# A chain of convolutions on one core: the first image's tables moved into its second convolution, the last image's mix and stores reordered

## The reference, cut to what matters

```python
# L0: attention over the 4096 pixels of an image, then three convolutions
qkv = batchnorm(x) @ w_qkv + b_qkv            # q, k centred, squared, normalised
attn = (v + q2 @ (k2.T @ v) / 64) @ w_ln + b_ln
y = leaky_relu(conv1x1(concat(attn, x), w1))  # conv1, 96 -> 96
y = leaky_relu(conv3x3(y, w2))                # conv2, 96 -> 96
x = conv1x1(y, w3) + x                        # 96 -> 48
# L1: separable convolution
x = batchnorm(pointwise(depthwise3x3(relu(x))))
# L2: weights mixed per image from 4 experts
rw = sigmoid(mean(x, (1, 2)) @ Wr + br)       # routing, 4 numbers
h = relu(bn1(x @ mix(rw, Wpw)))               # expansion, 48 -> 192
h = relu(bn2(depthwise3x3(h, mix(rw, Wdw))))  # 192 channels
x = bn3(h @ mix(rw, Wpwl)) + x                # projection, 192 -> 48
# L3: like L1, with its own weights
```

## Time and profile before

| | us |
|---|---|
| median of 3 runs (1068.31 to 1069.65) | 1069.26 |
| the profiled execution | 1068.75 |
| its span, first to last instruction | 1066.9 |
| TensorE busy in the span | 983.1 (92%) |
| VectorE busy | 877.0 (82%) |
| ScalarE busy | 473.4 (44%) |
| GpSimd busy | 94.7 (9%) |

### The profile page before, as it was taken

One profiled execution on the slowest core, in us unless ns is written; L12 is line 12 of the kernel. 1 busy time (PEld: TensorE's weight loads), 2 busy tenths in 40 slices (PEclk: granted clock), 3 DMA queues, 4 the chain that ended last, 5 costly groups with the idle time before them and its releaser, 6 DMA issues.

```text
span 1066.9 us, 14764 instructions
## 1 busy us (share of the span) xinstructions
PE 983.1 (92%) x4598; PEld 625.9 (59%) x4598; DVE 877.0 (82%) x1231; ACT 473.4 (44%) x813; POOL 94.7 (9%) x120
## 2 busy tenths in 40 slices
PE   5689879998999999998999999998999999998986
PEld 3456655665665666665665566665665676654624
DVE  6762579998699968999699978999599978997980
ACT  3311445255624635345533636355632646333522
POOL 0210002001300103001300003001200013000000
PEclk9799989999999999999999999999999999998998
DMA  5242815185526565175534656175533756145215
GB/s 73 50 122 50 142 31 143 30 134 127 115 76 96 106 130 139 35 120 126 126 81 82 119 116 151 35 120 112 123 98 71 131 118 150 36 91 118 60 30 102
DMA packets 129520, 104.48 MB, mean 98 GB/s; under 512 B 97903, under 2 KB 98772, under 8 KB 129492
## 3 DMA queue, kind: packets, MB, share of 16 engines
q1 hardware_dynamic: 129492, 104.14, 47.4%
HBM read 10.82 MB, written 6.29 MB: 16 GB/s over the span
## 4 chain that ended last, share of the span: by engine, by line
PE 54%; DVE 23%; issue 10%; SPq 6%; DMA 4%; ACT 2%; DVEq 0%; ACTq 0%
PE bank L1299 26%; DVE dwa L709 9%; PE bank L1279 5%; PE bank L1305 4%; PE bank L1331 4%; SPq L1007 3%; DVE a_parts L802 3%; PE bank L1346 3%; DMA y_parts<-a_parts 3%; PE bank L1347 2%; PE bank L1269 2%; DVE dwa L725 2%; PE bank L1315 2%; DVE dwb L725 2%; DVE s L627 1%
## 5 line engine op out<-in xcount | busy, mean ns | idle before, releaser
L709 DVE SCALAR_TENSOR_TENSOR dwa<-h1a,dyn,dwa 128x1024 f32<-128x1024 f32 x224 | 281.5, 1277 | 1.0
L1299 PE MATMUL bank<-y_parts,w_l 128*96 128x512 f32 x576 | 151.2, 407 | 0.0
L1299 PE MATMUL bank<-y_parts,w_h 128*96 128x512 f32 x576 | 147.8, 400 | 0.0
L709 DVE SCALAR_TENSOR_TENSOR dwb<-h1b,dyn,dwb 128x1024 f32<-128x1024 f32 x112 | 143.0, 1276 | 0.5
L1331 PE MATMUL bank<-a_parts,wt_h 128*112 128x512 f32 x384 | 117.2, 413 | 12.7 <-DMA y_parts<-a_parts 12.1
L1299 PEld LDWEIGHTS bank<-y_parts,w_l 128*96 128x96 f32 x576 | 91.4, 163 | 61.0 <-issue 22.0
L1299 PEld LDWEIGHTS bank<-y_parts,w_h 128*96 128x96 f32 x576 | 93.2, 162 | 44.6 <-issue 0.2
L1331 PEld LDWEIGHTS bank<-a_parts,wt_h 128*112 128x112 f32 x384 | 64.3, 176 | 47.8 <-issue 26.1
L1156 POOL TENSOR_TENSOR y_low<-y,y_parts 96x512 fp32r<-96x512 f32 x56 | 67.2, 1200 | 237.3 <-DVE y L763 237.3
L1149 POOL TENSOR_TENSOR tok<-tok,u 128x1536 f32<-128x1536 f32 x8 | 22.9, 2866 | 562.3 <-DVE u L629 562.3
L1279 PE MATMUL bank<-xq,w_cur 97*96 97x512 f32 x128 | 68.4, 616 | 3.7 <-DVE y L763 3.7
(11 more groups left out here) (265 smaller groups left out, 1656.3 us busy)
## 6 DMA issues: line engine op xcount, KB each, us to landing
y_parts<-y_parts SPq DMA_DIRECT2D x32, 396.0 KB, 3.5
y_parts<-a_parts SPq DMA_DIRECT2D x64, 198.0 KB, 3.0
y_parts<-a_parts SPq DMA_DIRECT2D x64, 197.6 KB, 3.5
tok<-in_x_dram SPq DMA_DIRECT2D x48, 192.0 KB, 4.9
y_parts<-y_low SPq DMA_DIRECT2D x64, 132.0 KB, 3.3
a_parts<-a_parts SPq DMA_DIRECT2D x128, 66.0 KB, 2.4
x_even<-y_parts SPq DMA_DIRECT2D x32, 198.0 KB, 3.7
x_odd<-y_parts SPq DMA_DIRECT2D x32, 198.0 KB, 4.0
```

Of the source, the lines that this page charges most:

```text
L709: nc.vector.scalar_tensor_tensor(out=dst, in0=tap_input(n, t), scalar=weight, in1=dst, op0=ALU.mult, op1=ALU.add).then_inc(tap_step, 1)
L1299: nc.tensor.matmul(bank[0:C2, :], wgt[:, t, :], y1_parts[:, part, rows, cols], start=part + t == 0, stop=False)
```

## The change

In the first image, three clears of VectorE move from ahead of the norms to just ahead of `conv1_out`; the column transposes and bias products of TensorE move from ahead of conv2 to behind its chunks 0 and 1; and `mix_weights` moves ahead of the query norms. In the last image, `mix_weights` moves ahead of the last two depthwise steps of the image before; TensorE does the halo and expansions 0 to 3 ahead of projection 3; ScalarE in place of VectorE evacuates the halo and banks 0 and 1; the low parts of L3's quarters 2 and 3 move behind `mix_project` and into the last depthwise run; ScalarE issues the copies of the last L3 quarter and a quarter of the last image's bytes, and the stores are split in halves by tokens.

```diff
...
                     step(nc.vector.memset(tile[:, :, :].bitcast(F32), 0.0))
+
+            def prepare_places():
+
                 step(nc.vector.memset(beside_f, 0.0))
                 step(nc.vector.memset(h1b[:, 0:PAIRS + 2:PAIRS + 1, :], 0.0))
                 step(nc.vector.memset(h1b[:, :, 0:WP:WP - 1], 0.0))
...
                     sums_out(attn)
+                    mix_weights(f)
                     norms_of_q(attn)
-                    mix_weights(f)
                     mix_project(f)
                     project_weights()
...
                 x2_low_part(f, 3)
                 depthwise_at(back, BY_PROJECT + 5, steps=slice(1, 4))
                 route(f)
-                depthwise_at(back, BY_PROJECT + 5, steps=slice(4, None))
+                depthwise_at(back, BY_PROJECT + 5, steps=slice(4, 5))
                 mix_weights(f)
+                depthwise_at(back, BY_PROJECT + 5, steps=slice(5, None))
+                dve.wait_ge(h1b_ready, H1B_WRITES * f + 4)
+                h1b_rows(f, 2)
+                h1b_rows(f, 3)
+                mix_project(f)
                 l3_low_part(back, 2)
-                halo_out(f)
-                h1b_rows(f, 0)
-                l3_low_part(back, 3)
-                for n in range(1, 4):
-                    h1b_rows(f, n)
-                mix_project(f)
                 dve.wait_ge(project_done, 2 * PCHUNKS * f)
                 project_weights()
                 dve.wait_ge(h1b_ready, H1B_WRITES * (f + 1))
                 third, fourth = LAST_STEPS.index((4, 5)), LAST_STEPS.index((4, 8))
-                depthwise_last(slice(0, third))
+                depthwise_last(slice(0, 4))
+                l3_low_part(back, 3)
+                depthwise_last(slice(4, third))
                 l3_low_part(f, 0)
                 depthwise_last(slice(third, fourth))
...
             conv1_weights(0)
+            prepare_places()
             conv1_out(0, None)
             prepare_norms()
             prepare_pairs()
...
-        def store(sp, image, chunks=range(4)):
+        def store(sp, image, chunks=range(4), steps=range(STEP)):
             wait(sp, ot_ready, 4 * image + chunks.stop)
+            store_chunks(sp, image, chunks, steps)
+
+        def store_chunks(queue, image, chunks, steps):
             dst = out[image].rearrange("(i j b) w c -> j b w i c", j=STEP, b=2)
             runs = slice(chunks.start * RUN // 4, chunks.stop * RUN // 4)
-            for j in range(STEP):
+            for j in steps:
                 src = ot_of(image)[j * W:(j + 1) * W, :].rearrange("p (b i c) -> p b i c", b=2, c=C)
                 for par in range(2):
-                    sp.dma_start(dst[j, par][:, runs, :], src[:, par, runs, :]).then_inc(stored, 16)
+                    queue.dma_start(dst[j, par][:, runs, :], src[:, par, runs, :]).then_inc(stored, 16)
...
-            beside_l3(sp, LAST, IMAGES)
-            store(sp, LAST, range(3))
-            store(sp, LAST, range(3, 4))
+            beside_l3(sp, LAST, IMAGES, range(PCHUNKS - 1))
+            store(sp, LAST, range(2))
+            store(sp, LAST, range(2, 4), steps=(0,))
             sp.wait_ge(stored, 16 * STORES * (IMAGES + 1))
...
-            def conv2(image):
...
                     last.then_inc(conv2_done, 1)
                     if k >= 2 and k % 2 == 0:
                         w3(image, k // 2 - 1)
+                    if first and k == 0:
+                        prepare_columns()
+                    if first and k == 1:
+                        prepare_biases()
...
-                conv2(f)
+                conv2(f, first=back is None)
...
                 routing(f)
-                project(back, (2, 3), begun=True)
+                project(back, (2,), begun=True)
                 expand_halo(f)
-                for n in range(6):
+                for n in range(4):
+                    expand(f, n)
+                project(back, (3,), begun=True)
+                for n in range(4, 6):
                     expand(f, n)
                 for m in range(1, PCHUNKS):
                     l3(back, (m,))
@@ -1505,8 +1520,6 @@
...
             conv1(0, None)
-            prepare_columns()
-            prepare_biases()
             iteration(0, 1, None)
...
+            def first_h1b_rows(f):
+
+                bias = dyn_of(f)[:, Y_B1 + 1:Y_B1 + 2]
+                act.wait_ge(expand_done, 13 * f + 1)
+                for n, (half, r) in enumerate(((slice(0, M2), PAIRS + 1), (slice(M2, M1), 0))):
+                    nc.scalar.activation(h1b[half, r, 1:W + 1], ring_b.bank(B_HALO)[half, n * W:(n + 1) * W], ACT.Relu,
+                                         bias=bias[half, :]).then_inc(h1b_ready, 1)
+                for n in range(2):
+                    act.wait_ge(expand_done, 13 * f + n + 2)
+                    nc.scalar.activation(h1b[:, 1 + n:2 * ROWS + n:2, 1:W + 1],
+                                         ring_b.bank(B_E + n)[:, :].rearrange("p (j w) -> p j w", w=W), ACT.Relu,
+                                         bias=bias).then_inc(h1b_ready, 1)
...
                 route(f)
                 finish_unit(back, 4)
+                act.wait_ge(weight_chain.sem, weight_chain.each * (f + 1))
+                first_h1b_rows(f)
                 finish_unit(back, 5)
                 project_affine(back, f + 1, 2)
                 project_affine(back, f + 1, 3)
-                act.wait_ge(weight_chain.sem, weight_chain.each * (f + 1))
                 h1a_rows(f, 4)
                 h1a_rows(f, 5)
...
                 last_finish(4)
                 taps_out(2)
+                project_affine(f, IMAGES, 2)
                 last_finish(5)
-                project_affine(f, IMAGES, 2)
                 project_affine(f, IMAGES, 3)
+                act.wait_ge(al3_ready, PCHUNKS * IMAGES)
+                copy_beside(act, L3, PCHUNKS - 1)
                 l3_out(f, (0,))
                 l3_and_tokens_out(f, range(1, PCHUNKS))
                 tokens_out(f, (PCHUNKS - 1,))
+                act.wait_ge(ot_ready, 4 * IMAGES)
+                store_chunks(act, f, range(2, 4), (1,))
...
```

1 line of the change is left out of this document (added).

## The result

The changed kernel takes 1083.66 us, median of 4 executions (1082.09 to 1085.71), against 1068.78 (1068.29 to 1069.65) for the kernel before: ratio 1.0135, 95% interval 1.0122 to 1.0148, 14.9 us slower. The direction was forecast; 1075.0 and its range up to 1079.6 were not enough. The profiled execution took 1083.47.

The account below looks back on a forecast made before the run. The chain was taken to run through VectorE and TensorE, with SyncE's stores at the end. Terms +2.1 + 1.7 + 0.3 + 5.2 + 0.5 - 3.3 = +6.5 us on 1068.75 gave 1075.0, range 1069.2 to 1079.6.

Parts of the forecast that it names:

- the queue in conv2: First image: chunk 2 waits for a bank emptied only after tables, biases and prepare_pairs; starts at 74.2, +2.1 us.
- the restart: First image, conv2's chunk 2: after TensorE's 7.6 us wait its clock restarts at the lower level, +1.7 us.
- the late low part of quarter 2: Last image: it ends at 983.3 instead of 977.0, so L3's quarter 1 starts 4.6 us late.
- all points from the first expansion to quarter 1: Last image: expansions start at 973.8, low part 2 ends at 983.3, quarter 1 starts at 990.3.
- the clears' term: First image: with three clears moved away, the norms start 1.50 us earlier, at no cost ahead of conv1's first result.
- I take +0.5, near nothing, since quarter 1's copies are out of the way earlier: Last image's end: ScalarE issuing quarter 3's copies beside SyncE's quarter 2 costs +0.5 us, bounds 0 and 3.66.
- a rival (3.66): Last L3 copies collide: quarter 2 lands 3.66 us late, total 1078.4, or 1079.6 with slow expansions; chance 0.14.
- the restart ahead of quarter 1: Last image: after some 6 us of standing, TensorE's clock restarts ahead of L3's quarter 1, +1.7 us.
- the stores: End: two queues issue the stores, last issue at 1060.4 plus 3.2 to the end, 1063.6; -3.3 us.
- the second image: Mix ahead of the query norms must wait for ScalarE's expert weights: +0.3 us.
- The first rival: Last image: quarter 1 isn't late and VectorE's gain of 2.8 less 0.7 counts; 1065.8 to 1067.5, chance 0.12.

Follow-up runs that it names:

- experiment 1: Changed kernel with ScalarE's affine of quarter 2 ahead of its h1b rows and VectorE's low parts of quarters 2 and 3 ahead of the last depthwise run: 1078.99 us.
- experiment 3: Changed kernel with the first image's column transposes and bias products back ahead of conv2: 1077.66 us.
- experiment 7: Changed kernel with the first image's column transposes ahead of conv2 and the bias products behind its chunk 0: 1074.34 us.
- experiment 8: Changed kernel with 28 unused matmuls on TensorE in its pause ahead of chunk 2 of the first image's conv2: 1078.08 us.
- Experiment 5: Kernel before with only the three clears moved to just ahead of conv1's evacuation: 1067.49 us, ratio 0.9974.
- experiment 2: Changed kernel with SyncE issuing all copies of the last image's L3, stores still on two queues: 1079.63 us.
- experiment 10: Kernel before with only the copies of the last image's last L3 quarter issued by ScalarE: 1072.89 us, ratio 1.0033.
- experiment 6: Kernel before with only the stores split in halves of tokens and issued on two queues: 1064.94 us, ratio 0.9959.
- experiment 12: Kernel of experiment 11 plus, in the last image, the mix ahead of the last two steps with nothing behind it late: 1053.53 us, ratio 0.9858.
- experiment 11: Kernel before with clears moved, bias products behind conv2's chunk 0, stores on two queues, low part ahead of the reciprocal: 1052.74 us, ratio 0.9841.

## Why the prediction was wrong

*Right, with their sizes:* the queue in conv2 (from chunk 0 to chunk 2 19.1 us, forecast 18.7; the pause 7.72, forecast 7.6; the restart 1.7), the late low part of quarter 2, and in the last image all points from the first expansion to quarter 1 within 0.2 us. Experiments 1, 3, 7 and 8 undid these one by one. That chunk 2 came at 73.55, forecast 74.2, was in part luck: the clears gave 1.1 us less than forecast, and a conv1 at the high clock gave back more than that. Experiment 5, whose norms begin at 26.63, shows the clears' term right.

*The step that failed* is "I take +0.5, near nothing, since quarter 1's copies are out of the way earlier". What collides is not quarter 1 but quarters 2 and 3 themselves. I had the price as a rival (3.66), and chose the low bound without a row for it; and I left out what follows from a late quarter, the restart, though I had priced one twice elsewhere. Measured: quarter 2 starts 3.5 later after quarter 1 and lasts 2.2 longer by the restart, 5.7 in place of 0.5. Of the 8.3 us by which the sum fell short of the traces this is 5.2, and with it alone the forecast would have been past its own range. Experiments 2 and 10 show it from both sides. The Trainium skill (DMA: Bandwidth & Descriptors, Issuing engines are not separate DMA queues) says that transfers issued by several engines run interleaved on the same 16 engines, and that only the time to initiate them is saved; the trace agrees, with twelve issues in 5.5 us instead of 8.3 and the last landing of all after 11.14 instead of 11.05.

*Sizes that were off:* the restart ahead of quarter 1, 2.6 (6.19 for the quarter, 996.10 to 1002.29, instead of 3.57) where I took 1.7 from conv2; the stores, where the last issue begins at 1077.58 and needs 4.1 to the end, not 3.2; the second image, +1.5 and not +0.3. Two slips of arithmetic weigh little: 74.2 - 72.17 is 2.0, not 2.1, and 139.48 - 139.12 is nearer 0.4 than 0.3. The first rival's 2.8 less 0.7 for the last depthwise run comes out of its rows as 3.8 less 0.7; the run did start 3.2 us earlier (983.6 and 986.8), and gained nothing, since VectorE then waited 5.29 and 3.11 us within it.

*Not of the change:* the 2.2 us of image 7. One profiled execution of before held a lucky 0.69, and I summed against its time. In the traces of experiments 5, 6 and 10, all built on before, it takes 3.34 there too. Without it and the -0.8 of the transfers in image 2 the change costs some 13.4 us. The ratio's interval doesn't part these.

## What to carry to other kernels

When a step is moved later in an engine's row, price what waits for it on the other engines, and add a restart of TensorE's clock to each long pause that this opens: those of 7.72, 6.58 and 3.45 us here cost 1.7, 2.6 and 2.2 us. A second issuing engine came with a gain at the last stores, where issues stood in line behind the last tokens; for the copies of two quarters it brought no landing of the later one forward, made the earlier one share, and nearly doubled its last landing. An instruction that takes 0.69 us in one image and 3.34 in another is worth a look at what starts with it on the other engines: one swap here gained 13.3 us, nearly as much as the whole change lost.

## What the runs showed of the hardware

- VectorE and GpSimd held each other for a whole instruction: 0.69 became 3.34, or 2.80 became 3.35. GpSimd's recorded start was the earlier one in all 66, by 4 and 5 ns where VectorE won and by 6 to 64 ns where it lost.
- With the copies of two quarters issued at once from two engines, the last copy of the earlier quarter landed after 7.07 and 7.12 us (after, experiment 10); with one engine issuing them in turn, after 3.66 and 3.65 (before, experiment 2).
- TensorE's clock does not follow the pause alone: after pauses of 2.57, 2.56 and 2.70 us at the same place chunk 2's first 18 matmuls took 4.5, 6.1 and 6.0 us (experiments 7, 12 and 11). The granted clock was 1.00 in all three pauses; then it stayed there, fell to 0.74 and 0.68 over the first and second nine matmuls, or fell to 0.54 over the first nine alone. The first expansions of the last image took 0.63 us a matmul in the traces of both kernels and 0.40 in that of experiment 8. What else decides it stays open, and with it some 2 us of each trace.
